# Scores issued ahead of the weighted values on TensorE, five copies of the values, and the key copy ahead of the logits' copy on ScalarE

## The chip, the cores and the metric

The kernel runs on one core of one Trainium2 chip. Its time is the device time in microseconds (us) of one execution; the median of three runs before the change is 304.14 us (303.58 to 305.31). The profile used below is of one execution of 303.86 us, whose first and last instruction lie 302.0 us apart.

## The reference

The kernel computes a gated cross-attention block followed by a gated mixture of eight experts, for 64 sequences of 64 rows of 128 numbers:

```
q = rope(layernorm(x) @ Wq.T + bq);  k = rope(ctx @ Wk.T + bk);  v = ctx @ Wv.T + bv      # 16 heads of 8
p = softmax(where(mask == 0, -1e9, q @ k.T / sqrt(8)))
x = x + tanh(g_xattn) * ((p @ v) @ Wo.T + bo)
y = layernorm(x);  logits = y @ Wr + br;  e = argmax(logits);  gate = softmax(logits)[e]
x = x + tanh(g_ffn) * gate * (gelu(y @ W1[e] + b1[e]) @ W2[e] + b2[e])
```

## The kernel before

**Tiling.** The 4096 rows are 32 tiles (T) of 128 rows, two sequences each. The attention of a tile is spread over seven steps of a software pipeline: every engine runs the same loop of steps, in step i it works on tile i for the projections and on older tiles for the later stages, and semaphores join the engines. Each engine executes its own list strictly in the order written in its `step(i)`; nothing reorders it. From step 34 on the expert layers follow, 39 sorted tiles of rows, gathered from a table in memory (`rows`).

**The stages of attention, with their lines.** In step i:

- TensorE (PE in the profile): projections of tile i (L763 to L765, `ps_qx` and `ps_kv`); transposes of the stacked queries and keys of tile i-1 (L778); weighted values of tile i-4, probabilities times values (L788, called pv below), into `ps_o`; scores of tile i-2 (L803), used only for the row maxima; transpose of the normalised output of i-5 (L815); the scores again, transposed and with the maxima taken off, of tile i-3 (L827 and L830, into `ps_st`); output projection of i-5 (L843, L844); transpose of the maxima of i-2 (L854). The projections of the next tile follow.
- VectorE (DVE): normalises the output of i-5 (L1144, L1147); queries with bias of tile i (L1157); residual and statistics of i-6 (L1172 to L1180); row maxima of the scores of i-2 (L1212, `mx`); splits the rotated queries and keys of tile i into halves (L1223, L1224, `stk`). Five groups of tiles are routed to experts in between (steps 11 to 14, 18 to 21, 25 to 28 and later).
- ScalarE (ACT): exponentials of i-4 (L589, `pr`); copy of the transposed maxima of i-3 (L595, `mxT`); copy of the router's part of tile i, eight columns (L605, the logits' copy); keys of tile i (L609, `qk`, the key copy); mask row (L613); keys and queries of i-1 out of PSUM (L623 `kT`, L626 `qT`); four copies of the values of tile i (L637, `vx`); output of i-5 (L643).
- GpSimd (POOL): the low halves of the stack of tile i-1 (L526); scatter of finished rows (L512, steps 15 to 31); the rotary embedding of tile i (L539, L541, L545).
- SyncE (SP): for tile i-1 four DMAs that copy `kT` into a block-diagonal form, `kbd` (L406). The scores L803 and L830 read `kbd`. SP also issues the input and weight loads (weights at steps 4, 7, ... 25, columns, context and rows at 3, 5, 6, 9 and so on), behind the four of the step.

**What joins them.** The scores of tile t wait for the four DMAs of `kbd` (`kbd_ld`), for `qT` and for the maxima of tile t-1 (`mx_done`, since `ps_s` is one buffer). pv of tile t waits for the exponentials (`p_rdy`), for the values (`v_ev`) and for the normalisation of tile t-1 (`on_done`). L778 waits for the halves of the stack (`hi_done`, `lo_done`) and for the copies of older maxima (`mxT_ev`). The exponentials wait for L830 (`st_done`). `kbd`, `qT` and `vx` are rings of four (`RING = 4`): the value copy of tile t waits until pv of tile t-4 is done.

Of the kernel before, what the change touches and what calls it, by code (L numbers as in the profile page):

```python
# [12 lines left out]
ACT = mybir.ActivationFunctionType  # L13
# [3 lines left out]
P = 128  # L17
B, S, D = 64, 64, 128
H, HD = 16, 8
T = B * S // P  # L20
NE, FF = 8, 512
FC = FF // P
NS = T + NE - 1
NA = 4
# [4 lines left out]
EPS = 1e-5  # L29
OUT_OF_RANGE = 8192  # L30
RING = 4
GOT = 20
W_SCALE = 64.0
QX = D + NE
ROW = 144
R_LOGIT, R_MEAN, R_VAR, R_STD, R_GATE, R_ID = 128, 136, 137, 138, 139, 140
# [54 lines left out]
def wait(eng, sem, n):  # L91

    if n > 0:
        eng.wait_ge(sem, n)
# [7 lines left out]
def build(nc, x, ctx_t, mask, g_x, g_f, Wq, bq, Wk, bk, Wv, bv, Wo, bo, W1, W1r, W2, b2, Wr, br,  # L102
          x_t, WoN, const_f, const_h, const_i, rows, out):
    stack = ExitStack()
    with stack:
        def sb(name, shape, dt=F32):
            return stack.enter_context(nc.sbuf_tensor(name, shape, dt))
# [56 lines left out]
        x_all = sb("x_all", [P, T, ROW])  # L164
# [12 lines left out]
        kT = sb("kT", [P, 2, NA, P], F16)  # L177
        qT = sb("qT", [P, RING, NA, P], F16)
        kbd = sb("kbd", [P, RING, 2, 2 * NA, 2, S], F16)
        vx = sb("vx", [P, RING, 2, 8, 32])  # L180
        mx = sb("mx", [P, 2, P], F16)
        mxT = sb("mxT", [P, 2, P], F16)
        pr = sb("pr", [P, 2, 8, 2, S])
# [50 lines left out]
        ps_s = ps[1]  # L234
# [7 lines left out]
        ps_lx = bank[6][:, D:QX]  # L242
# [69 lines left out]
        def live(t):  # L312
            return 0 <= t < T
# [257 lines left out]
        def _(act):  # L571
# [12 lines left out]
            def step(i):  # L584
# [16 lines left out]
                t = i  # L601
                if live(t):
                    par, s = t % 2, t % RING
                    act.wait_ge(qe_ev, t + 1)
                    act.activation(x_all[:, t, R_LOGIT:R_LOGIT + NE], ps_lx, ACT.Copy).then_inc(lx_ev, 1)  # L605
                    if t == 0:
                        act.wait_ge(s_mb, 2)
                    wait(act, rope2, t - 1)
                    act.activation(qk[:, par, D:2 * D], ps_kv[:, 0:D], ACT.Identity, scale=mask_s[:, t:t + 1]).then_inc(k_ev, 1)  # L609
                    if t == 0:  # L610
                        act.wait_ge(s_z1, 5)
                    wait(act, stk_done, t - 1)
                    act.activation(k_stack(par)[:, :, ROW_MASK], mask_b[:, t:t + 1].broadcast_to([P, H]), ACT.Copy  # L613
                                   ).then_inc(mrow, 1)
# [12 lines left out]
                                   ).then_inc(qT_ev, 1)  # L627
                t = i
                if live(t):
                    s = t % RING  # L630
                    wait(act, pv_done, t - RING + 1)
                    if t == 0:
                        act.wait_ge(s_v1, 2)
                    v_ps = ps_kv[:, D:2 * D].rearrange("p (j hh d) -> p j hh d", hh=2, d=HD)
                    for b in range(2):
                        for hh in range(2):
                            act.activation(vx[64 * hh:64 * hh + 64, s, b, :, 16 * hh:16 * hh + HD],  # L637
                                           v_ps[64 * b:64 * b + 64, :, hh, :], ACT.Copy).then_inc(v_ev, 1)
# [25 lines left out]
        def _(pe):  # L664
# [84 lines left out]
            def step(i):  # L749
# [17 lines left out]
                if live(t):  # L767
                    par = t % 2
                    pe.wait_ge(hi_done, 2 * t + 2)
                    pe.wait_ge(lo_done, t + 1)  # L770
                    pe.wait_ge(mrow, t + 1)
                    wait(pe, mxT_ev, t - 1)
                    wait(pe, qT_ev, t)
                    for w in range(2):
                        first = w * (H * STK + 8)
                        for a in range(NA):
                            c = (w * NA + a) * P
                            mm = pe.transpose(ps_stk[:, c:c + P], stk[:, par, first + a * P:first + a * P + P], ident_h)  # L778
                    mm.then_inc(stk_done, 1)
                t = i - 4  # L780
                if live(t):
                    s, par = t % RING, t % 2
                    pe.wait_ge(p_rdy, t + 1)
                    pe.wait_ge(v_ev, t * 4 + 4)
                    wait(pe, on_done, t)
                    for j in range(8):
                        for b in range(2):
                            mm = pe.matmul(ps_o[S * b:S * b + S, 32 * j:32 * j + 32], pr[:, par, j, b, :], vx[:, s, b, j, :],  # L788
                                           start=True, stop=True)
                    mm.then_inc(pv_done, 1)  # L790
                if tile(i - F0):
                    rows_transposed(i - F0)
                if tile(i - F0 - 1):
                    first_layer(i - F0 - 1)
                t = i - 2
                if live(t):
                    s = t % RING
                    pe.wait_ge(kbd_ld[s], (t // RING) * 64 + 64)
                    pe.wait_ge(qT_ev, t + 1)
                    wait(pe, mx_done, t)  # L800
                    for a in range(NA):
                        for b in range(2):
                            mm = pe.matmul(ps_s[S * b:S * b + S, 2 * P * a:2 * P * a + 2 * P], qT[:, s, a, S * b:S * b + S],  # L803
                                           kbd[:, s, :, 2 * a + b, :, :].rearrange("p w h k -> p w (h k)"),
                                           start=True, stop=True)
                    mm.then_inc(s_done, 1)
                t = i - 5
                if live(t):
                    if t == 0:
# [488 lines left out]
```

## Time and profile before

| | us |
|---|---|
| median of 3 runs | 304.14 (303.58 to 305.31) |
| profiled execution | 303.86 |
| its span, first to last instruction | 302.0 |
| TensorE busy | 238.8 (79%) |
| VectorE busy | 191.4 (63%) |
| ScalarE busy | 166.5 (55%) |
| GpSimd busy | 182.0 (60%) |
| mean granted TensorE clock | 0.955 |

The attention takes roughly the first 200 us and the experts the rest. In the full steps of attention (38 to 175 us) all four compute engines are busy for most of the time, so a step is set by chains that pass through several engines. Times in the views are from the span's start. A row of the timeline merges instructions of a line that follow each other (x8: eight of them); the brackets give the engine's idle time before it and what ended that.

### The profile page before, as it was taken

To read this page: it belongs to the slowest core of one execution; us is meant where nothing else is said; L and a number is where in the kernel's file an instruction comes from. 1 tells how busy PE (TensorE), PEld (TensorE's weight loads), DVE (VectorE), ACT (ScalarE), POOL (GpSimd) and SP (SyncE) were. 2 spreads that over 40 slices of the span, in tenths; PEclk is the share of its full clock that TensorE was granted. 3 is DMA by queue.
4 is the path that set the end of the run, shared out by engine and by line. 5 is a ranking of instruction groups with operands and counts; after the bars stand their busy time and mean duration, and the time that the engine had idled before them with its cause. 6 is when DMAs were issued, how large, how long until landed. Compare 5 with 4: busy or idle time off the path is not lost.

```text
span 302.0 us, 10491 instructions
## 1 busy us (share of the span) xinstructions
PE 238.8 (79%) x3529; PEld 207.8 (69%) x3529; DVE 191.4 (63%) x639; ACT 166.5 (55%) x481; POOL 182.0 (60%) x222
## 2 busy tenths in 40 slices
PE   1358889997998887888889967866676899999960
PEld 1236667876887676677677846755565899999960
DVE  5545858889898889977798684754452444444420
ACT  2145577887877875687786852352512444444410
POOL 7466665659468885488967766036473445555560
PEclk9999999999999999999999995799877999999995
DMA  7711465446454724143521212411134322200100
GB/s 221 218 17 25 103 177 124 125 114 185 108 136 114 200 59 135 25 126 66 137 46 37 47 36 71 109 33 40 59 107 112 100 65 61 74 29 31 37 19 0
DMA packets 58536, 26.63 MB, mean 88 GB/s; under 512 B 38609, under 2 KB 53990, under 8 KB 58485
## 3 DMA queue, kind: packets, MB, share of 16 engines
q1 hardware_dynamic: 55204, 20.15, 27.7%
q0 software_dynamic: 2272, 4.46, 4.4%
q10 hardware_dynamic: 1008, 1.35, 1.5%
q8 instruction: 31, 0.51, 0.7%
q14 instruction: 21, 0.16, 0.2%
HBM read 16.70 MB, written 5.51 MB: 74 GB/s over the span
## 4 chain that ended last, share of the span: by engine, by line
PE 35%; DVE 13%; POOL 13%; issue 12%; ACT 7%; SPq 6%; DMA 5%; another core or an unknown queue 4%; POOLq 1%; DVEq 0%; ACTq 0%
PE ps L745 11%; SPq L406 5%; PE ps L788 4%; DMA kbd<-kT 3%; POOL rot L545 3%; POOL rot L539 3%; POOL rot_s L541 3%; PE ps L728 2%; PE ps L726 2%; PE ps L727 2%; PE ps L803 2%; DVE mx L1212 2%; ACT pr L589 2%; DMA x_all<-in_x 2%
## 5 line engine op out<-in xcount | busy, mean ns | idle before, releaser
L560 POOL DMA_INDIRECT out<-fin,got x39 | 37.7, 967 | 37.5 <-DVE fin L1261 26.4
L1212 DVE TENSOR_REDUCE mx<-ps 128x16 f16<-128x1024 f32 x32 | 39.1, 1222 | 19.1 <-PE ps L803 15.1
L745 PE MATMUL ps<-w_f,hT 128*128 x312 | 46.8, 295 | 0.0
L512 POOL DMA_INDIRECT rows<-x_all,dest_i x32 | 33.3, 1040 | 21.4 <-DVE x_all L1062 14.3
L1261 DVE SCALAR_TENSOR_TENSOR fin<-ps,got 128x128 f32<-128x128 f32 x39 | 13.6, 350 | 46.9 <-PE ps L745 33.1
L788 PE MATMUL ps<-vx,pr 128*64 128x32 f32 x1024 | 37.3, 227 | 4.1 <-DVE on L1147 2.4
L745 PEld LDWEIGHTS ps<-w_f,hT 128*128 128x128 f32 x312 | 39.7, 199 | 0.8
L788 PEld LDWEIGHTS ps<-vx,pr 128*64 128x64 f32 x1024 | 33.8, 142 | 8.0 <-issue 2.9
L589 ACT ACTIVATE pr<-ps 128x1024 f32<-128x1024 f32 x32 | 32.7, 1023 | 8.7 <-PE ps L830 8.2
L539 POOL TENSOR_TENSOR rot<-qk,cf 128x256 f32<-128x256 f32 x32 | 23.5, 734 | 22.1 <-ACT qk L609 16.3
L657 ACT ACTIVATE hT<-ps 128x512 f32<-128x512 f32 x39 | 23.3, 597 | 23.2 <-PE ps L728 16.2
L526 POOL TENSOR_TENSOR stk<-rot,stk 128x256 f16<-128x256 f32 x32 | 21.6, 675 | 23.4 <-DVE stk L1224 23.4
L830 PE MATMUL ps<-qT,kbd 128*128 128x64 f16 x512 | 33.7, 195 | 0.7 <-issue 0.7
L827 PE MATMUL ps<-mxT,ch 128*128 128x128 f16 x256 | 33.7, 223 | 0.0
L830 PEld LDWEIGHTS ps<-qT,kbd 128*128 128x128 f16 x512 | 31.5, 100 | 1.5 <-issue 1.1
L778 PEld LDWEIGHTS ps<-ch,stk 128*128 128x128 f16 x256 | 16.0, 101 | 22.9 <-issue 18.4
L778 PE MATMUL ps<-ch,stk 128*128 128x128 f16 x256 | 20.7, 227 | 13.1 <-POOL stk L526 10.2
L726 PE MATMUL ps<-gT,w_h 128*128 128x128 f16 x156 | 30.0, 227 | 0.0
L727 PE MATMUL ps<-gT,w_h 128*128 128x128 f16 x156 | 29.9, 226 | 0.0
L728 PE MATMUL ps<-gT,w_l 128*128 128x128 f16 x156 | 29.8, 226 | 0.0
L637 ACT ACTIVATE vx<-ps 64x64 f32<-64x64 f32 x128 | 27.9, 218 | 2.5
L600 ACT ACTIVATE gT<-ps 128x128 f16<-128x128 f32 x39 | 10.8, 277 | 31.0 <-PE ps L714 23.4
(156 smaller groups left out, 604.6 us busy)
## 6 DMA issues: line engine op xcount, KB each, us to landing
kbd<-kT SPq DMA_DIRECT2D x128, 32.0 KB
got<-rows SPq DMA_DIRECT2D x39, 72.0 KB
w_f<-in_W_rows SPq DMA_DIRECT2D x8, 256.0 KB, 2.9
w_r<-in_W_last_row SPq DMA_DIRECT2D x8, 256.0 KB, 4.1
w_f<-in_L_ffn_W SPq DMA_DIRECT2D x8, 256.0 KB
x_all<-in_x SPq DMA_DIRECT2D x3, 512.0 KB, 4.7
xt_all<-in_x_t SPq DMA_DIRECT2D x3, 512.0 KB, 4.3
ct_all<-in_ctx SPq DMA_DIRECT2D x3, 512.0 KB, 4.3
```

The costliest lines, as they stand in the source:

```text
L512: pool.indirect_dma_start(out=rows, out_offset=bass.IndirectOffsetOnAxis(ap=dest_i[:, t:t + 1], axis=0), in_=x_all[:, t, :], in_offset=Non ...
L560: pool.indirect_dma_start(out=out_d, out_offset=bass.IndirectOffsetOnAxis(ap=got_i[:, u % GOT, R_ID:R_ID + 1], axis=0), in_=fin[:, u % FRI ...
L589: act.activation(pr[:, t % 2, :, :, :].rearrange("p j b q -> p (j b q)"), ps_st[:, :], ACT.Exp, scale=SCALE).then_inc(p_rdy, 1)
L726: pe.matmul(o, w_h, gT[:, par, 0, :], start=True, stop=False)
L727: pe.matmul(o, w_h, gT[:, par, 1, :], start=False, stop=False)
L728: mm = pe.matmul(o, w_l, gT[:, par, 0, :], start=False, stop=True)
L745: mm = pe.matmul(o, hT[:, par, c, :], w2_f[:, bass.ds(e, 1), c, :].rearrange("p o n -> p (o n)"), start=False, stop=(c == FC - 1))
L778: mm = pe.transpose(ps_stk[:, c:c + P], stk[:, par, first + a * P:first + a * P + P], ident_h)
L788: mm = pe.matmul(ps_o[S * b:S * b + S, 32 * j:32 * j + 32], pr[:, par, j, b, :], vx[:, s, b, j, :], start=True, stop=True)
L827: pe.matmul(ps_st[:, P * j:P * j + P], sel_h[:, j, :], mxT[:, par, :], start=True, stop=False)
L830: mm = pe.matmul(ps_st[:, c:c + S], kbd[:, s, j % 2, 2 * (j // 2) + b, :, :].rearrange("p h k -> p (h k)"), qT[:, s, j // 2, S * b:S * b + ...
L1212: dve.tensor_reduce(mx[:, t % 2, 0:H], ps_s[:, :].rearrange("p (h k) -> p h k", k=S), AX.X, ALU.max).then_inc(mx_done, 1)
```

## The change

Three edits. TensorE issues the scores of tile i-2 directly behind the transposes of tile i-1 and ahead of pv of tile i-4; the order of all else on it stays. The values get a ring of five buffers (`VRING = 5`), so that the copy of tile t waits for pv of tile t-5. ScalarE makes the key copy ahead of the logits' copy; the wait on `qe_ev` now stands ahead of the key copy.

```
+VRING = 5
-        vx = sb("vx", [P, RING, 2, 8, 32])
+        vx = sb("vx", [P, VRING, 2, 8, 32])
...
                     act.wait_ge(qe_ev, t + 1)
-                    act.activation(x_all[:, t, R_LOGIT:R_LOGIT + NE], ps_lx, ACT.Copy).then_inc(lx_ev, 1)
                     if t == 0:
                         act.wait_ge(s_mb, 2)
                     wait(act, rope2, t - 1)
                     act.activation(qk[:, par, D:2 * D], ps_kv[:, 0:D], ACT.Identity, scale=mask_s[:, t:t + 1]).then_inc(k_ev, 1)
+                    act.activation(x_all[:, t, R_LOGIT:R_LOGIT + NE], ps_lx, ACT.Copy).then_inc(lx_ev, 1)
...
-                    s = t % RING
-                    wait(act, pv_done, t - RING + 1)
+                    s = t % VRING
+                    wait(act, pv_done, t - VRING + 1)
...
+                t = i - 2
+                if live(t):
+                    s = t % RING
+                    pe.wait_ge(kbd_ld[s], (t // RING) * 64 + 64)
+                    pe.wait_ge(qT_ev, t + 1)
+                    wait(pe, mx_done, t)
+                    for a in range(NA):
+                        for b in range(2):
+                            mm = pe.matmul(ps_s[...], qT[...], kbd[...], start=True, stop=True)
+                    mm.then_inc(s_done, 1)
                 t = i - 4
                 if live(t):
-                    s, par = t % RING, t % 2
+                    s, par = t % VRING, t % 2
                     pe.wait_ge(p_rdy, t + 1)
...
-                t = i - 2
-                if live(t):
...
-                    mm.then_inc(s_done, 1)
```

On TensorE, one step of attention before the change, from the projections (`wqx`, `wkv`, `bk_h`) through the stack's transposes (`stk`), pv (`vx,pr`) and the scores (`kbd,qT`) to the transpose of the output (`on`):

```order
L763 MATMUL ps<-wqx,xt_all 128x136 [waits router_part_copied,v_copied]
L764 MATMUL ps<-wkv,ct_all 128x256
L765 MATMUL ps<-bk_h,ch 128x128
L778 MATMUL ps<-ch,stk 128x128 [waits max_copied,mask_row_made,qT_copied,lo_made,hi_made]
L778 MATMUL ps<-ch,stk 128x128 x7
L788 MATMUL ps<-vx,pr 64x32 [waits o_normalised,v_copied,probs_made]
L788 MATMUL ps<-vx,pr 64x32 x15
L803 MATMUL ps<-kbd,qT 64x256 [waits max_made,qT_copied,kbd_loaded3]
L803 MATMUL ps<-kbd,qT 64x256 x7
L815 MATMUL ps<-cf,on 128x128 [waits x2_made,o_normalised]
```

The same place after it (the lines are one higher, and the scores are now L789, pv is L801):

```order
L764 MATMUL ps<-wqx,xt_all 128x136 [waits router_part_copied,v_copied]
L765 MATMUL ps<-wkv,ct_all 128x256
L766 MATMUL ps<-bk_h,ch 128x128
L779 MATMUL ps<-ch,stk 128x128 [waits max_copied,mask_row_made,qT_copied,lo_made,hi_made]
L779 MATMUL ps<-ch,stk 128x128 x7
L789 MATMUL ps<-kbd,qT 64x256 [waits max_made,qT_copied,kbd_loaded3]
L789 MATMUL ps<-kbd,qT 64x256 x7
L801 MATMUL ps<-vx,pr 64x32 [waits o_normalised,v_copied,probs_made]
L801 MATMUL ps<-vx,pr 64x32 x15
L816 MATMUL ps<-cf,on 128x128 [waits x2_made,o_normalised]
```

The scores with their wait for the DMAs of `kbd` have moved ahead of the 16 products of pv; what stands in front of and behind the pair is the same.

On ScalarE, one step before the change, from the exponentials (`pr`) to the copies of the values (`vx`):

```order
L589 ACTIVATE pr<-ps 128x1024 [waits pv_made,scoresT_made]
L595 ACTIVATE mxT<-ps 128x128 [waits scoresT_made,max_transposed]
L605 ACTIVATE x_all<-ps 128x8 [waits q_scaled]
L609 ACTIVATE qk<-ps,mask_s 128x128 [waits rope_sin]
L613 ACTIVATE stk<-mask_b 128x16 [waits stacks_transposed]
L623 ACTIVATE kT<-ps 128x512 [waits kbd_loaded3,stacks_transposed]
L626 ACTIVATE qT<-ps 128x512 [waits scoresT_made]
L637 ACTIVATE vx<-ps 64x8x8 [waits pv_made]
```

And after it:

```order
L590 ACTIVATE pr<-ps 128x1024 [waits pv_made,scoresT_made]
L596 ACTIVATE mxT<-ps 128x128 [waits scoresT_made,max_transposed]
L609 ACTIVATE qk<-ps,mask_s 128x128 [waits rope_sin,q_scaled]
L610 ACTIVATE x_all<-ps 128x8
L614 ACTIVATE stk<-mask_b 128x16 [waits stacks_transposed]
L624 ACTIVATE kT<-ps 128x512 [waits kbd_loaded3,stacks_transposed]
L627 ACTIVATE qT<-ps 128x512 [waits scoresT_made]
L638 ACTIVATE vx<-ps 64x8x8 [waits pv_made]
```

The key copy (`qk`) and the logits' copy (`x_all`) have changed places; the copy of the values still waits for pv, now for that of the tile five back.

## Rows read from the trace of the kernel before

**Rows 1.** The page: busy us, share of the span, instructions by engine.
```profile
PE 238.8 (79%) x3529; PEld 207.8 (69%) x3529; DVE 191.4 (63%) x639; ACT 166.5 (55%) x481; POOL 182.0 (60%) x222
```

**Rows 2.** Stretches: length, busy time (x instructions) by engine, granted clock, DMA share, GB/s.
```profile
38.00:63.00 25.00, 22.46 (x408) 19.01 (x404) 19.69 (x61) 20.05 (x64) 15.02 (x21) 1.00 0.53 133
175.00:200.00 25.00, 19.08 (x329) 16.37 (x330) 16.42 (x63) 9.63 (x25) 8.58 (x11) 0.80 0.29 66
```

**Rows 3.** Timeline of one full step (start us, us, engine line).
```profile
62.50 0.61 PE L778 MATMUL ps<-ch,stk 128*128 128x128 f16 x8 [0.45 <-ACT mxT L595]
63.04 1.12 PE L788 MATMUL ps<-vx,pr 128*64 128x32 f32 x32
63.99 0.61 PE L803 MATMUL ps<-kbd,qT 128*64 128x256 f16 x8
...
65.81 1.02 ACT L589 ACTIVATE pr<-ps 128x1024 f32<-128x1024 f32 x1 [0.35 <-PE ps L830]
65.95 0.22 PE L854 MATMUL ps<-ch,mx 128*128 128x128 f16 x1
...
66.35 0.67 POOL L526 TENSOR_TENSOR stk<-rot,stk 128x256 f16<-128x256 f32 x1 [1.02 <-DVE stk L1224]
...
66.73 0.27 ACT L595 ACTIVATE mxT<-ps 128x128 f16<-128x128 f16 x1
66.76 0.22 PE L765 MATMUL ps<-bk_h,ch 128*128 128x128 f16 x1
...
67.26 0.44 PE L778 MATMUL ps<-ch,stk 128*128 128x128 f16 x5 [0.28 <-POOL stk L526]
```

**Rows 4.** Waits of 26 to 180 us: us in total, times, longest.
```profile
DVE mx L1212 <- PE ps L803: 12.7, 15, 1.4
ACT pr L589 <- PE ps L830: 5.8, 17, 0.4
PEld ps L803 <- DMA kbd<-kT: 2.6, 3, 1.2
PE ps L803 <- DMA kbd<-kT: 2.2, 2, 1.1
```

**Rows 5.** Timeline: a step whose scores wait for the DMAs.
```profile
102.90 0.61 PE L778 MATMUL ps<-ch,stk 128*128 128x128 f16 x8 [0.28 <-POOL stk L526]
...
105.70 0.63 PE L803 MATMUL ps<-kbd,qT 128*64 128x256 f16 x8 [1.13 <-DMA kbd<-kT]
...
108.98 0.22 PE L778 MATMUL ps<-ch,stk 128*128 128x128 f16 x1 [0.28 <-POOL stk L526]
```

**Rows 6.** The chain of waits near 20 us (start us, us): an issue, its landing, the scores.
```profile
20.60 1.98 DMA kbd<-kT
...
22.62 1.08 PE ps L803 x8
```

**Rows 7.** Timeline of SP: the four issues of kbd for tiles 7 and 9.
```profile
54.16 3.39 SPq L406 DMA_DIRECT2D kbd<-kT  x4
63.90 2.55 SPq L406 DMA_DIRECT2D kbd<-kT  x4
```

**Rows 8.** Timeline of TensorE: the scores of those two tiles.
```profile
59.06 0.61 PE L803 MATMUL ps<-kbd,qT 128*64 128x256 f16 x8
68.75 0.61 PE L803 MATMUL ps<-kbd,qT 128*64 128x256 f16 x8
```

**Rows 9.** Timeline of a step set by GpSimd (132 to 139 us).
```profile
132.19 0.67 POOL L526 TENSOR_TENSOR stk<-rot,stk 128x256 f16<-128x256 f32 x1 [0.61 <-DVE stk L1224]
132.96 0.61 PE L778 MATMUL ps<-ch,stk 128*128 128x128 f16 x8 [0.80 <-POOL stk L526]
...
137.29 0.66 POOL L526 TENSOR_TENSOR stk<-rot,stk 128x256 f16<-128x256 f32 x1
```

**Rows 10.** Timeline of the last scores of attention.
```profile
188.15 1.02 ACT L589 ACTIVATE pr<-ps 128x1024 f32<-128x1024 f32 x1 [1.18 <-PE ps L830]
...
189.26 1.92 PE L788 MATMUL ps<-vx,pr 128*64 128x32 f32 x32 [0.37 <-ACT pr L589]
...
190.96 1.07 PE L803 MATMUL ps<-kbd,qT 128*64 128x256 f16 x8
```

More of the change, by code:

```diff
@@ L779, in step @@
                     mm.then_inc(stk_done, 1)
+                t = i - 2
[6 more added lines that the diff above has]
+                        for b in range(2):
+                            mm = pe.matmul(ps_s[S * b:S * b + S, 2 * P * a:2 * P * a + 2 * P], qT[:, s, a, S * b:S * b + S],
+                                           kbd[:, s, :, 2 * a + b, :, :].rearrange("p w h k -> p w (h k)"),
+                                           start=True, stop=True)
+                    mm.then_inc(s_done, 1)
                 t = i - 4
                 if live(t):
-                    s, par = t % RING, t % 2
+                    s, par = t % VRING, t % 2
                     pe.wait_ge(p_rdy, t + 1)
@@ L794, in step @@
                     first_layer(i - F0 - 1)
-                t = i - 2
-                if live(t):
[L797 to L805, printed above, removed]
-                    mm.then_inc(s_done, 1)
                 t = i - 5
```

## The prediction

> **What bounds the kernel now.** I read the page's busy shares first [rows 1]: no engine fills the span, so a step of attention is set by a chain. The stretches [rows 2] then show where: TensorE is busy for 22.46 of 25 us between 38 and 63 us, and its clock is granted in full. Next the timeline of one undisturbed step [rows 3]: the transposes L778 start at 62.50 and again at 67.26, so a step is 4.76 us. Three chains lead from one to the other.
>
> Chain A, through ScalarE: L778, pv, scores and the transposed scores run back to back on TensorE until the exponentials can start at 65.81 (3.31 us). They end at 66.83, the copy of the maxima L595 behind them ends at 67.00, and L778 starts at 67.26: 3.31 + 1.02 + 0.17 + 0.26 = 4.76. The wait table confirms it: the exponentials waited for L830 17 times between 26 and 180 us [rows 4].
>
> Chain B, through VectorE and GpSimd: L778, pv, scores, maxima, the two halves of the stack, L526 (ends 67.02), L778. In the steps where L526 was the last thing waited for L778 comes 0.10 us behind its end (132.86, 132.96) [rows 9], so this chain needs 67.12 - 62.50 = 4.62 us [rows 3].
>
> Chain C is TensorE's own work: L778 at 62.50 to the end of L765 at 66.98, 4.48 us, including the 0.22 us that the last product drains.
>
> The timeline names L526 as the last releaser of L778 by 0.02 us, but both are within a hair; what matters is that A stands at the full 4.76.
>
> **Moving the scores.** It removes nothing and adds no instruction. In chain A both pv and scores lie between L778 and L830, in whichever order: the swap takes nothing out of it. In chain B pv drops out, 63.99 - 63.04 = 0.95 us; but B is only level with A, so while A stands the gain is between 0 and 4.76 - 4.62, and I take 0. The 15 waits of the maxima for the scores, 12.7 us [rows 4], look like the gain of this change; yet behind the maxima in many of those steps VectorE waits again, for the rotary embedding, and in the rest TensorE comes to the maxima's transpose L854 when its own list allows (65.95 above, 0.08 us behind the maxima's end).
>
> The price is the cover of a DMA. The scores wait for the four `kbd` transfers of their tile, and pv of an older tile, which needs none of them, was executed during that wait. An in-order TensorE now stands still with pv behind the wait; the output transpose, L830, the exponentials and the next L778 are all queued behind pv. In the step at 102.90 pv ran right behind L778 and the scores waited till 105.70, 1.13 us idle [rows 5]. With the swap the scores still start at 105.70, pv starts about 0.5 us later than them, and L830 comes 0.95 us later than before.
>
> How much cover each tile has left: a landing comes 1.37 us behind the end of its last issue at the least (20.60 + 1.98 = 22.58, the issue itself being 0.61 us) [rows 6]. For tile 9 the issues end at 66.45, so it has landed at 67.82, and the scores started at 68.75: 0.93 us to spare, just the 0.95 that is needed. For tile 7 the issues end at 57.55, landed 58.92, scores at 59.06: 0.1 us to spare [rows 7, 8]. The same subtraction for all tiles 2 to 29 gives six with nothing to spare (2, 4, 5, 11, 16, 22; five of these waits are visible, 4.8 us [rows 4]), three with 0.1 (7, 8, 27), ten with 0.4 to 0.98 (3, 6, 9, 13, 14, 15, 17, 23, 25, 28), and the rest with enough.
>
> What of it reaches the end. A stall lengthens its own step, and the next tile's `kbd`, issued relative to the step's start, then has that much more time; so 5 falls in the shadow of 4 and 8 in that of 7. The delays of L778 by tile: Tile 2: 0.95, of which about 0.45 lies in a step that waited for L526 and had that room: +0.5. Tiles 4, 11, 16: +0.75, +0.8, +0.95 = +2.5 (what tile 2 gave the next steps is taken off). Tile 5: +0.2. Tiles 7 and 27: 0.85 each, less 0.1 of room in the first: +1.65. Tile 22: 0.95, but steps 22 to 26 are set by GpSimd (scatter, rotary embedding, L526 in a ring of 137.29 - 132.19 = 5.1 us [rows 9], whatever TensorE does) and TensorE catches up: 0. The ten with partial cover: their missing parts come to about 2 us, most of it eaten by the room that an earlier stall made: +0.6.
>
> Together +5.45. The bounds of this term: only the visible waits outside the GpSimd-bound steps, four times 0.95 halved by room, 1.9 us; or all cover lost with nothing eaten, (6 x 0.95) + (3 x 0.87) + 2.0 = 10.3 us.
>
> The Trainium skill ("DMA: Bandwidth & Descriptors", Rules for kernel authors) says to issue a DMA early, compute, and wait on its semaphore late; this change waits earlier for the same issue. By that rule every transfer would lose cover, which is the upper bound, 10.3 us; the rows agree with it for tile 7 and leave tile 9 almost untouched [rows 7, 8], so the sum above stands.
>
> **The tail.** At 188.15 to 189.17 TensorE waits for the exponentials and then does pv and the scores of tile 31 (189.26, 190.96) [rows 10]. With the swap these scores run in the gap. They take 1.07 us there, at the lower clock; I take -0.9 us (0 to -1.07). The scores of tile 30 have landed too late to gain.
>
> **Five value buffers.** Before, pv ends at 64.16 just before the values' copy; with pv 0.5 us later a ring of four would make ScalarE wait that long in front of the value copies and the next projections. With five it waits for a pv a whole step old. So this edit removes a cost of the first one and gives nothing by itself: 0. The larger memset (one quarter more) lies in the start-up, and what it delays, GpSimd's zeroing of `kbd`, is needed only when the first `kbd` issue comes, many microseconds later: 0.
>
> **The key copy first.** The logits' copy holds ScalarE for about 0.07 us ahead of the key copy. GpSimd gets the keys 0.07 us earlier; where it was waiting for them and is on the path (about three steps) that gives -0.2 us. The logits' copy is needed by the next projections, behind the value copies on the same engine, so its delay costs 0.
>
> **Sum.** +5.45 - 0.9 - 0.2 = +4.35. VectorE's own long steps (routing; 102.90 to 108.98 is one of 6.1 us [rows 5]) will swallow a little more than I gave them; I take +4.0. On the profiled execution that is 303.86 + 4.0 = 307.9 us; the profiled time is 0.3 below the median of the runs, so I leave it at 307.9. The expert part is only shifted: its first tiles stand behind the last attention steps on every engine.
>
> **Rivals.**
> 1. The maxima's chain was the bound, and the stalls are small: A is only seemingly full (L595's 0.26 us to L778 could be a coincidence), B loses 0.95, and the step falls to chain C, 4.48. About 12 steps are at 4.76 to 4.83, so 12 x 0.28 = 3.4 us, and the tail 0.9. With stalls of 1.9 us: 303.86 - 3.4 - 0.9 + 1.9 = 301.5 us, faster. For it: L778's releaser is named L526 in this step, and the waits of the maxima are the largest on VectorE. Against it: the 17 waits of the exponentials [rows 4], and L778 never less than 0.25 us behind L595, 0.26 here [rows 3]. It decides from the point where the stalls come to less than about 2.8 us (303.86 - 4.3 + 2.8 is 1.8 below the median).
> 2. The stalls are hidden: the steps bound by VectorE and GpSimd swallow them all but two, and the tail gives back 0.9: 303.86 + 1.9 - 0.9 - 0.2 = 304.7 us, no change. For it: of 28 steps only about half are near 4.8 us.
> 3. All cover is lost, with late transfers made later by the longer queue: 303.86 + 10.3 - 1.1 = 313.1 us. Against: the shadowing above is plain arithmetic.
> 4. The clock falls. The step at 102.90 had 1.13 us of idle for `kbd` [rows 5], the longest such wait is 1.2 us [rows 4], and between 38 and 63 us the clock kept 1.00, while 175 to 200 us with its long waits has 0.80 [rows 2]. If two steps ran at the lower of the two levels (1.2 instead of 2.4 GHz), each would cost up to another 4.48 us: 307.9 + 9 = 317 us. [...]
>
> **Chances.** Forecast (3 to 6 us of loss) 0.6; rival 1 0.12; rival 2 0.15; rival 3 0.1; rival 4 0.03. A measurement here tells a change from none at about 0.5%, 1.5 us. Faster by more than that (under 302.6): 0.12. Within: 0.14. Slower (over 305.7): 0.74. The range 303.0 to 311.2 leaves out rival 1's 0.12 below, and rival 4 and part of rival 3 above. The forecast's own range is 305.7 to 310.
>
> **What would show it.** Right: the scores' waits for `kbd` grow from 4.8 us in 5 (26 to 180 us) to over 10 us in ten or more; pv follows the scores; the maxima's waits for the scores shrink to a few us while the exponentials still wait for L830 in about as many steps; undisturbed steps stay at 4.76. Steps at 4.5 us would show rival 1. The prediction is wrong if the pv that starts at 189.26 now [rows 10] starts no later than that.

## The result, and the profile after

On one chip, runs of the two kernels in turn: 308.6 us median after (306.25 to 309.22, 4 runs) against 303.86 before (302.93 to 305.31, 4 runs). The ratio is 1.0126, 95% interval 1.0076 to 1.0175, so the change costs 1.3%. Times in this document are medians of all runs and ratios compare the fast runs alone, which matters for the second timing of after: three of its six runs were slow, and it is 310.85 us over all six and 307.76 over the fast three. The profiled execution of after took 308.0 us (span 306.1, granted clock .943); that of before 303.86 (302.0, .955). A second pair of traces from another chip, called the repeats below, gives 309.54 against 304.71 us (spans 307.8 and 302.8).

The busy times of after, in the columns of [rows 1]:

```profile
PE 239.0 (78%) x3529; PEld 212.7 (69%) x3529; DVE 191.3 (62%) x639; ACT 164.6 (54%) x481; POOL 181.9 (59%) x222
```

As many instructions as before, and as busy, but for the weight loads (+4.9 us) and ScalarE (-1.9 us). The loss is waiting and clock. The wait table of after, 26 to 180 us, against [rows 4]:

```profile
PEld ps L789 <- DMA kbd<-kT: 13.4, 17, 1.4
ACT pr L590 <- PE ps L831: 9.8, 20, 0.9
PE ps L789 <- DMA kbd<-kT: 9.6, 13, 1.2
DVE mx L1213 <- PE ps L789: 4.0, 8, 1.0
```

The scores' wait for `kbd` has grown and the maxima's wait for the scores has shrunk, 12.7 to 4.0 us. These rows also show a mistake of mine: PEld and PE are the two halves of one stall (the load waits, and its matmul behind it), so they must not be added. Counted by the weight loads, before had 3 stalls of 2.6 us in all, not five of 4.8, and after has 17 of 13.4 us. The repeats say 3 of 1.4 and 15 of 10.7. Below I count by the weight loads alone, and call each such wait a stall.

One step with such a stall, that of tile 7's scores, against [rows 3] and the first row of [rows 8] (timeline of after; start, duration, engine line):

```profile
57.73 0.61 PE L779 MATMUL ps<-ch,stk 128*128 128x128 f16 x8 [0.31 <-ACT mxT L596]
...
59.27 0.63 PE L789 MATMUL ps<-kbd,qT 128*64 128x256 f16 x8 [0.93 <-DMA kbd<-kT]
...
59.73 1.07 PE L801 MATMUL ps<-vx,pr 128*64 128x32 f32 x32
59.94 1.23 DVE L1213 TENSOR_REDUCE mx<-ps 128x16 f16<-128x1024 f32 x1 [0.32 <-PE ps L789]
60.73 0.33 PE L816 MATMUL ps<-cf,on 128*128 128x128 f32 x1
...
62.01 1.02 ACT L590 ACTIVATE pr<-ps 128x1024 f32<-128x1024 f32 x1
62.93 0.27 ACT L596 ACTIVATE mxT<-ps 128x128 f16<-128x128 f16 x1
...
63.45 0.61 PE L779 MATMUL ps<-ch,stk 128*128 128x128 f16 x8 [0.31 <-ACT mxT L596]
```

TensorE stands for 0.93 us with pv queued behind the scores, and everything behind pv is that much later: from the transposes to the exponentials 62.01 - 57.73 = 4.28 us (3.31 in an undisturbed step of before), and the step takes 5.72 us instead of 4.76. The releaser of L779 is now ScalarE's copy of the maxima, in this step and in the undisturbed ones, which take 4.72 us.

The end of attention: the last scores (tile 31), with the exponentials and pv of their step (tile 29; timeline), against [rows 10]:

```profile
189.76 1.02 ACT L590 ACTIVATE pr<-ps 128x1024 f32<-128x1024 f32 x1 [1.18 <-PE ps L831]
```
```profile
190.43 1.06 PE L789 MATMUL ps<-kbd,qT 128*64 128x256 f16 x8
191.29 1.86 PE L801 MATMUL ps<-vx,pr 128*64 128x32 f32 x32
```

The scores of tile 31 do stand ahead of pv, but TensorE comes to them only at 190.43, 0.67 us behind the start of the exponentials, and pv then waits for nothing but its turn: 191.29 instead of 189.26.

How the two pairs part along the span. First the start of the last tile's transposes (timeline) in before and in its repeat:

```profile
180.51 0.61 PE L778 MATMUL ps<-ch,stk 128*128 128x128 f16 x8 [0.92 <-POOL stk L526]
```
```profile
179.96 0.61 PE L778 MATMUL ps<-ch,stk 128*128 128x128 f16 x8 [0.92 <-POOL stk L526]
```

and in after and in its repeat:

```profile
182.03 0.61 PE L779 MATMUL ps<-ch,stk 128*128 128x128 f16 x8 [0.85 <-POOL stk L527]
```
```profile
182.98 0.61 PE L779 MATMUL ps<-ch,stk 128*128 128x128 f16 x8 [0.85 <-POOL stk L527]
```

| us, after less before | first pair | repeats |
|---|---|---|
| last transposes of attention | +1.5 | +3.0 |
| from there to the end of the last exponentials | +0.2 | +1.7 |
| from there to the end of the span | +2.4 | +0.2 |
| span | +4.1 | +4.9 |

So 1.5 and 3.0 of the 4 to 5 us are lost by the last transposes, and the rest comes behind them. (The first transposes of after started 0.2 and 0.9 us earlier than those of before; counted from there, the attention steps cost 1.7 and 3.9 us.) The clock shows part of what comes behind. Stretches of the first trace of before (columns of [rows 2]):

```profile
202.00:230.00 28.00, 16.32 (x151) 14.73 (x151) 12.03 (x56) 9.00 (x19) 16.07 (x17) 0.88 0.22 68
230.00:240.00 10.00, 10.00 (x106) 9.89 (x106) 3.64 (x14) 3.78 (x9) 4.84 (x5) 0.83 0.46 118
```

and of the first of after:

```profile
202.00:230.00 28.00, 18.93 (x160) 17.02 (x159) 12.35 (x57) 9.34 (x18) 17.57 (x18) 0.82 0.20 64
230.00:240.00 10.00, 8.07 (x68) 7.98 (x68) 3.16 (x12) 3.28 (x8) 2.91 (x3) 0.66 0.38 102
```

In both stretches the first trace of after has less clock, 0.82 against 0.88 and 0.66 against 0.83. In the repeats it is another stretch, the end of attention itself; before, then after:

```profile
181.00:202.00 21.00, 16.91 (x270) 14.33 (x270) 12.69 (x51) 7.28 (x16) 6.46 (x7) 0.76 0.28 73
```
```profile
181.00:202.00 21.00, 17.52 (x222) 15.27 (x219) 11.75 (x43) 6.71 (x16) 6.71 (x7) 0.59 0.31 73
```

Between 184.6 and 201.6 us the repeat of after had the lower level, 1.2 GHz, without a break (the repeat of before from 182.4 to 192.6), and did 48 matmuls fewer in the 21 us.

### The profile page after: what moved, and what is told of

Read it like the earlier page. It is cut to its first block, busy times and chain, and to the rows that moved or that the text cites. A ratio compares the mean times of both kernels' runs of the same rounds, so it can differ in the third digit from the quotient of the medians.

```text
span 306.1 us, 10522 instructions
## 1 busy us (share of the span) xinstructions
PE 239.0 (78%) x3529; PEld 212.7 (69%) x3529; DVE 191.3 (62%) x639; ACT 164.6 (54%) x481; POOL 181.9 (59%) x222
## 3 DMA queue, kind: packets, MB, share of 16 engines
q10 hardware_dynamic: 1008, 1.35, 1.5%
## 4 chain that ended last, share of the span: by engine, by line
PE 45%; issue 12%; DMA 10%; SPq 9%; DVE 8%; ACT 6%; POOL 5%; another core or an unknown queue 2%; DVEq 0%; POOLq 0%; ACTq 0%
PE ps L746 13%; DMA kbd<-kT 8%; SPq L407 8%; PE ps L801 5%; PE ps L789 3%; PE ps L729 3%; PE ps L727 3%; PE ps L728 3%; PE ps L831 3%; PE ps L828 3%; ACT kT L624 2%; DVE mx L1213 2%; DMA x_all<-in_x 2%; PE ps L779 2%
## 5 line engine op out<-in xcount | busy, mean ns | idle before, releaser
L561 POOL DMA_INDIRECT out<-fin,got x39 | 37.8, 970 | 39.6 <-DVE fin L1262 29.1
L746 PE MATMUL ps<-w_f,hT 128*128 x312 | 48.9, 305 | 0.0
L746 PEld LDWEIGHTS ps<-w_f,hT 128*128 128x128 f32 x312 | 42.0, 209 | 0.8
L590 ACT ACTIVATE pr<-ps 128x1024 f32<-128x1024 f32 x32 | 32.7, 1023 | 13.4 <-PE ps L831 12.8
L801 PEld LDWEIGHTS ps<-vx,pr 128*64 128x64 f32 x1024 | 34.9, 141 | 1.5 <-ACT pr L590 1.5
L801 PE MATMUL ps<-vx,pr 128*64 128x32 f32 x1024 | 35.2, 223 | 0.9 <-ACT pr L590 0.9
L831 PE MATMUL ps<-qT,kbd 128*128 128x64 f16 x512 | 34.5, 197 | 1.0 <-issue 1.0
L779 PEld LDWEIGHTS ps<-ch,stk 128*128 128x128 f16 x256 | 16.0, 101 | 22.0 <-issue 18.2
L789 PE MATMUL ps<-kbd,qT 128*64 128x256 f16 x256 | 21.4, 292 | 12.2 <-DMA kbd<-kT 11.3
L779 PE MATMUL ps<-ch,stk 128*128 128x128 f16 x256 | 20.7, 227 | 12.2 <-POOL stk L527 5.5
```

Source lines behind the costliest of these rows:

```text
L561: pool.indirect_dma_start(out=out_d, out_offset=bass.IndirectOffsetOnAxis(ap=got_i[:, u % GOT, R_ID:R_ID + 1], axis=0), in_=fin[:, u % FRI ...
L590: act.activation(pr[:, t % 2, :, :, :].rearrange("p j b q -> p (j b q)"), ps_st[:, :], ACT.Exp, scale=SCALE).then_inc(p_rdy, 1)
L746: mm = pe.matmul(o, hT[:, par, c, :], w2_f[:, bass.ds(e, 1), c, :].rearrange("p o n -> p (o n)"), start=False, stop=(c == FC - 1))
L831: mm = pe.matmul(ps_st[:, c:c + S], kbd[:, s, j % 2, 2 * (j // 2) + b, :, :].rearrange("p h k -> p (h k)"), qT[:, s, j // 2, S * b:S * b + ...
```

## Experiments

Three groups of runs, each on one chip with the kernel before beside it. The chips are not equal: before took 288.78 us on the first, 304.2 on the second and 288.17 on the third, so only ratios, and the traces up to the end of attention, are carried from one to the other. "Last transposes" is the start of the last tile's, as above.

**The scores ahead, and nothing else.** The scores' block of before put ahead of pv; ring of four, logits' copy first.

```
@@ on TensorE, in the loop over i, behind the stack's transposes @@
+                t = i - 2
+                if live(t):
...                     (scores, as in the change)
                 (pv of tile i - 4)
-                t = i - 2
-                if live(t):
...
```

> The scores ahead of pv alone; ring of four and the logits' copy first, as before. Theory A (the scores' wait for kbd, with pv queued behind it, makes the loss; the ring of five takes away a second one): besides the kbd waits, ScalarE now waits for pv in front of the value copies, about 0.5 us, of which 0.15 to 0.3 us per undisturbed step comes through to the exponentials: last L778 at 183.5 to 186 us instead of 182.0, time 309.5 to 312. Rival (ring and key copy matter nothing): last L778 at 182 to 182.5, time 308 to 309.

Measured: 295.27 us, ratio 1.0231 (1.0188 to 1.0275). Last transposes:

```profile
184.23 0.61 PE L778 MATMUL ps<-ch,stk 128*128 128x128 f16 x8 [0.91 <-POOL stk L526]
```

Its waits, 26 to 180 us:

```profile
ACT vx L637 <- PE ps L800: 13.1, 24, 1.5
PEld ps L788 <- DMA kbd<-kT: 9.1, 15, 1.5
...
ACT pr L589 <- PE ps L830: 1.5, 1, 1.5
```

The move of the scores alone makes the loss, and more of it than the whole change (2.3% against 1.3 and 1.1%). The first row shows what the ring of five is for: with four, ScalarE's copies of the values wait for pv in 24 steps, 13.1 us, a row that does not exist in after. ScalarE becomes the late one, and TensorE almost never keeps the exponentials waiting (1 time instead of 17).

**Ring of five and key copy first, scores behind pv.** The changed kernel with the block put back.

```
@@ against the changed kernel @@
-                t = i - 2           (scores, ahead of pv)
...
                 (pv of tile i - 4)
+                t = i - 2           (scores, behind pv)
...
```

> The ring of five and the key copy first, the scores behind pv as before. Theory A: the kbd waits go back to 5 to 7 in number, last L778 at 180 to 180.5 us, time 303 to 304, as before or up to 0.5 us less. Rival B (the loss comes from the ring's memory or from ScalarE's order): last L778 at 181.5 or later, time 307 to 309.

Measured: 288.99 us, ratio 0.9982 (0.9943 to 1.0022). Waits, 26 to 180 us:

```profile
DVE mx L1213 <- PE ps L804: 13.8, 16, 1.7
...
PEld ps L804 <- DMA kbd<-kT: 2.7, 5, 0.7
```

No change in time that can be told, and nearly the wait table of before. The two smaller edits are neither loss nor gain together; the loss comes with the order of scores and pv.

**The changed order without the wait for `kbd`.** The scores of a tile read the block-diagonal keys of the tile before and wait for those, which have long landed (so the scores computed are another tile's).

```
@@ against the changed kernel @@
-                    pe.wait_ge(kbd_ld[s], (t // RING) * 64 + 64)
+                    o = max(t - 1, 0)
+                    r = o % RING
+                    pe.wait_ge(kbd_ld[r], (o // RING) * 64 + 64)
...
-    kbd[:, s, :, 2 * a + b, :, :]
+    kbd[:, r, :, 2 * a + b, :, :]
```

> The changed kernel, but the scores of tile t read the kbd of tile t-1 and wait for its landing, a step old (the maxima are those of other keys; all transfers are still made). Theory A: no wait for kbd in front of the scores, so the gains stay alone (2.8 us by the steps that got shorter, and 0.9 in the tail) with undisturbed steps at 4.72: last L778 at 176 to 178 us, time 299 to 302. Rival C (the wait is not the cost, pv being later in the step is): last L778 still at 181 to 182.5, time 307 to 309. Should the undisturbed step fall to 4.5 us, the maxima's chain was the bound after all.

Measured: 285.41 us, ratio 0.9865 (0.9821 to 0.9909). Last transposes, and one step (timeline):

```profile
176.59 0.61 PE L779 MATMUL ps<-ch,stk 128*128 128x128 f16 x8 [0.85 <-POOL stk L527]
```
```profile
60.58 0.61 PE L779 MATMUL ps<-ch,stk 128*128 128x128 f16 x8 [0.31 <-ACT mxT L596]
61.12 0.63 PE L791 MATMUL ps<-kbd,qT 128*64 128x256 f16 x8
61.58 1.07 PE L803 MATMUL ps<-vx,pr 128*64 128x32 f32 x32
...
63.85 1.02 ACT L590 ACTIVATE pr<-ps 128x1024 f32<-128x1024 f32 x1 [0.42 <-PE ps L833]
64.78 0.27 ACT L596 ACTIVATE mxT<-ps 128x128 f16<-128x128 f16 x1
...
65.30 0.61 PE L779 MATMUL ps<-ch,stk 128*128 128x128 f16 x8 [0.31 <-ACT mxT L596]
```

With the wait gone the same order is 1.35% faster than before instead of about 1.2% slower. So the loss comes from the wait for the DMAs in this order. But the step is 4.72 us, not 4.48: chain A is the bound, and rival 1's idea that TensorE alone would set the step is out.

**The same in the order of before.** The control for the run just told: the same edit, in before.

> The kernel before, scores behind pv, but reading the kbd of the tile one older and waiting for that landing (as in the third experiment). Theory A: the kernel before had most waits covered by pv, so this removes at most its 4.8 us of visible waits, of which 1 to 3 us reach the end: last L778 at 177.5 to 179.5 us, 0.3 to 1 per cent faster. Then the scores ahead of pv without a wait (176.6) are still ahead of it by 1 to 3 us, the gain of the order alone. Rival: the order gains nothing without the wait, and this kernel too ends its last L778 at 176.6.

Measured on the second chip: 303.42 us, ratio 0.9977 (0.9945 to 1.0009). Last transposes:

```profile
179.42 0.61 PE L778 MATMUL ps<-ch,stk 128*128 128x128 f16 x8 [0.92 <-POOL stk L526]
```

Before hardly loses anything by `kbd`. Against 179.42 the new order, freed of the wait, starts its last transposes at 176.59, 2.8 us earlier; I had taken that gain as 0. But it can't be put down to the order: four single steps are together 3.5 us shorter, and each has another reason in the traces. Two of them, 1.1 us together, stand at the start. TensorE is granted the higher clock level from 29.1 us here, and from 23.0 us in the run with the scores ahead. The transposes of tile 2, here and there:

```profile
26.44 1.06 PE L778 MATMUL ps<-ch,stk 128*128 128x128 f16 x8
```
```profile
25.93 0.61 PE L779 MATMUL ps<-ch,stk 128*128 128x128 f16 x8
```

The order is not what raises the clock: after has it from 29.2 us, and a run below whose first tiles are all in the order of before has it from 23.5. The third step, 1.55 us, holds a fall of the clock in this run, from 73.5 to 76.9 us (the step takes 6.28 us, in before and its repeat 4.81):

```profile
70.00:75.00 5.00, 3.33 (x53) 2.42 (x52) 3.93 (x13) 3.02 (x11) 4.11 (x5) 0.85 0.50 129
```

The fourth, 0.9 us, is told in the last section. So the two ratios, 0.9865 and 0.9977, say, each against before on its own chip, that without the wait the changed kernel is about 1% better; how much of that is the order's own is open.

**The repeats.** Both kernels unchanged, on the second chip.

> The kernel before itself, for its trace beside the other three. Last L778 at 180 to 181 us; the end wherever the granted clock and the transfers of this chip put it.

> The changed kernel itself, timed once more beside the kernel before on one chip. Theory A: last L778 1 to 2 us later than in the kernel before, ratio 1.004 to 1.016. Rival D (the first comparison's last 2.6 us, behind the attention, belong to the change too): ratio 1.012 or more, with the end 3.5 us or more later than before.

Measured: 304.71 us for the traced run of before (median of its 17 other runs 304.2); after 307.76, ratio 1.0106 (1.0047 to 1.0165). The ratio is in the expected range; the last transposes, 3.0 us later than in before, are not (1 to 2 expected). Waits of the repeat of before, 26 to 180 us:

```profile
DVE mx L1212 <- PE ps L803: 11.3, 15, 1.2
PEld ps L803 <- DMA kbd<-kT: 1.4, 3, 0.7
```

and of the repeat of after:

```profile
PEld ps L789 <- DMA kbd<-kT: 10.7, 15, 1.3
...
DVE mx L1213 <- PE ps L789: 3.0, 7, 0.7
```

The pattern is stable, single steps are not. The step with tile 4's scores went from 5.97 to 5.50 us in the first pair and from 5.31 to 5.65 in the repeats; the step that ends with the transposes of tile 26 from 4.80 to 5.05 and from 4.79 to 6.09.

**The scores ahead only where the transfer has landed.** Tiles whose landing left room in before go ahead of pv, the others stay behind.

```
@@ against the changed kernel; scores(t) is its block made a function @@
+            FIRST = (6, 9, 10, 12, 15, 18, 19, 20, 21, 24, 26, 29, 30, 31)
...
+                if live(i - 2) and i - 2 in FIRST:
+                    scores(i - 2)
                 (pv of tile i - 4)
+                if live(i - 2) and i - 2 not in FIRST:
+                    scores(i - 2)
```

> The changed kernel, with the scores ahead of pv only for tiles 6, 9, 10, 12, 15, 18 to 21, 24, 26 and 29 to 31, whose kbd had landed 0.9 us or more before the scores in the kernel before; behind pv for the others. Theory A: hardly a loss (under 0.5 us), part of the gain: last L778 at 178.5 to 180 us, time 301 to 303.5. Rival C: half of the loss stays, last L778 at 181, time 305 to 307.

> The fourth experiment's kernel again (scores ahead of pv only for the fourteen tiles whose kbd is early), beside the kernel before on one chip. Theory A: last L778 1.5 to 2.5 us earlier than before, ratio 0.990 to 0.998.

Measured: 287.62 us, ratio 0.9958 (0.9921 to 0.9994), on the first chip, and 286.92, 0.9972 (0.9938 to 1.0007), on the third. Waits of the first, 26 to 180 us, and its last transposes:

```profile
DVE mx L1220 <- PE ps L760: 8.6, 12, 1.4
PEld ps L760 <- DMA kbd<-kT: 4.1, 7, 1.2
```
```profile
178.28 0.61 PE L794 MATMUL ps<-ch,stk 128*128 128x128 f16 x8 [0.84 <-POOL stk L527]
```

The loss is gone and some 0.3 to 0.4% is gained, at the edge of what can be told from nothing: the fastest version in which each tile's maxima come from its own scores, if only just. Attention gained more than that: the last transposes start at 178.28 here and at 176.50 in the second trace (1.5 to 2.5 us earlier than in before was expected, 3.5 to 4.0 came). Yet the last exponentials end at 192.06 and 192.08 us. In the second trace VectorE waits for the first rows that were gathered for the experts, and the normalisation that pv needs stands behind that wait in its list:

```profile
186.09 0.34 DVE L1139 TENSOR_SCALAR z<-got 128x127 f32<-128x127 f32 x1 [1.03 <-DMA got<-rows]
```

So an attention that ends early can be held up by the next stage's transfers. How much of the 1.8 us between the two traces went that way was not tested.

**Are the loads of the experts' second weights why `kbd` comes late?** SP issues them in the same steps. One step later (against the changed kernel):

```
+                if i - 1 in EXPERT_AT:
+                    e = EXPERT_AT[i - 1]
                     sp.dma_start(w2_f[:, e, :, :], ...
```

> The changed kernel, with the second layer's weights (256 KB each, the last of three loads that SP issues behind kbd in steps 4, 7, ... 25) issued one step later. Theory A: kbd of tiles 4, 7, 10, 13, 16, 22 lands late because these loads fill the queue; a third of them moved away makes those landings up to 1 us earlier, but the next tile's later: waits for kbd fall from 23 us to 17 to 21, last L778 at 180.5 to 181.8 us, time 0 to 1.5 us less than the changed kernel. Rival: landings are late for SP's own issue time (2.5 to 3.4 us for four), then nothing changes.

Measured: 310.65 us, ratio 1.0217 (1.0174 to 1.0259); 15 stalls, 12.2 us; last transposes at 184.09. Not better than the changed kernel on that chip (1.0106) but worse, so this expectation failed. Why it is worse was not found; its trace also has the lower clock level from 76.6 to 80.0 us, which after does not. Then all of them behind attention, in the changed kernel and in the selective one:

```
-                    sp.dma_start(w2_f[:, e, :, :], ...
...
+                if i == T:
+                    for e in range(NE):
+                        sp.dma_start(w2_f[:, e, :, :], ...
```

> The changed kernel, with all eight loads of the second layer's weights issued in step 32, behind the last kbd. A third of the bytes of the weight loads is then gone from steps 4 to 25 instead of moved by a step. If these loads make kbd land late (theory A): waits of the scores for kbd from 20 to 26 us down to 12 to 18, last L778 at 180 to 181.5 us; the total is open, since 2 MB now land while the first gathered rows do. Rival: SP's issue time alone makes kbd late, then waits stay within 1 us of the changed kernel and last L778 is at 182 to 183.

> Both together: scores ahead of pv for the fourteen tiles, second layer's weights at step 32. Last L778 at 176.5 to 178.5 us; ratio to the kernel before 0.985 to 0.997, if the late weights don't hold the first expert tiles up; if they do, 1.00 to 1.01.

Measured: 298.01 us, ratio 1.0377 (1.0321 to 1.0433), and 294.34, ratio 1.022 (1.0169 to 1.027). The times say little: SP now issues these loads ahead of the first gathers of rows for the experts, and in the first of the two VectorE waits 6.1 us for the first of those rows. The second was expected at 0.985 to 0.997, or at 1.00 to 1.01 if the experts were held up; it came out worse than both. The waits of the first, 26 to 180 us, and its last transposes:

```profile
PEld ps L791 <- DMA kbd<-kT: 10.8, 17, 1.1
```
```profile
180.56 0.61 PE L781 MATMUL ps<-ch,stk 128*128 128x128 f16 x8 [0.84 <-POOL stk L529]
```

With none of those loads in attention there are still 17 stalls, 10.8 us (after 17 and 13.4, its repeat 15 and 10.7). So these loads are not why TensorE stalls. The last transposes come 1.5 and 2.4 us earlier than in after and its repeat, which is what the expectation wanted to see if the loads did matter; 0.9 us of that is again the step of the last section. In 12 of the 17 stalls `kbd` landed 1.34 to 1.36 us behind the end of its last issue, about the shortest time seen: there the cover is short by the issue and the landing of `kbd` themselves. In the other five it landed 1.6 to 2.7 us behind, and why was not found. Tile 9 in before: its transposes start at 62.50 [rows 3], its four issues are the quickest there are, 2.55 us to 66.45 [rows 7], and land 1.37 us later, at 67.82: 5.32 us. Scores ahead of pv come one step and 0.54 us behind the transposes, 4.72 + 0.54 = 5.26 us. So the new order has no room at all in an undisturbed step, and there every issue slower than 2.55 us, and every later landing, stalls TensorE.

**Does a delay late in attention cost more than itself?** Before, with the scores of tile 28 made five times over (same values).

```
@@ against before @@
+                    for _ in range(5 if t == 28 else 1):
                         for a in range(NA):
...
```

> The kernel before, with the eight score matmuls of tile 28 made five times instead of once: 32 more matmuls, 1.84 us more on TensorE in one step of attention and no other change. It asks what a delay at the end of attention costs in the total. If the expert part is only shifted: last L778 1.4 to 1.9 us later, the total 1.4 to 2.2 us more (ratio 1.005 to 1.007). Rival D (a later attention also makes the transition and the clock's windows cost more): total 2.8 us or more (ratio 1.009 or more).

Measured: 290.37 us, ratio 1.008 (1.0045 to 1.0115), that is +2.3 us (1.3 to 3.3) for a step that grew from 4.76 to 6.50, +1.74 us. Both expectations overlap the interval: neither is excluded, and other steps of its trace were longer too (its last transposes start at 183.50, 3.0 us later than in before, and its clock was at the lower level from 75.9 to 79.3 us). That a lost us late in attention costs more than one stays open.

## Why the prediction was right, step by step

The total was right: 307.9 forecast, 308.6 measured on the first chip and 307.76 on the other, both inside 303.0 to 311.2. So was the mechanism: the cover of the `kbd` transfers is lost. Its terms were not all right, and that they sum to the right total is partly luck, as errors cancelled: attention was priced too dear, what lies behind it at nothing.

- **The removed cover.** Shown. Scores alone: 1.0231. Without the wait: 0.9865. All nine tiles named with no more than 0.1 us to spare (2, 4, 5, 7, 8, 11, 16, 22, 27) wait in the trace of after and in its repeat; of the ten with partial cover 13, 14, 17, 23, 25 and 28 wait too in the first, and beside them 20 and 29. Subtracting the landing from the start of the scores, tile by tile, is a good forecast of who waits. Two things it had too simple. 1.37 us from the last issue to the landing is about the least (1.34), not the rule: tiles 4, 5, 16 and 17 landed 2.3 to 3.6 us behind it in before, and the prediction's own list holds only with their real landings. And the move is 0.95 us only where pv starts at once. In the step of tile 29's scores pv itself had waited for VectorE in before, 1.27 us up to 176.19, so these scores moved forward by about 2.2 us, and a tile that was counted as safe waits in both traces of after.
- **The wait rows.** Mis-read: "five of these waits are visible, 4.8 us" was three, 2.6 us, shown twice. It entered only the lower bound: by its own rule three times 0.95 halved, 1.4 us instead of 1.9.
- **+5.45 for attention** was too much. By tiles, first pair: the step of tile 2 +0.47 (forecast +0.5), of 7 +0.80 and of 27 +0.79 (together +1.65 forecast, +1.59 measured), 4 and 5 together +0.13 (+0.95), 16 -0.35 (+0.95), 22 +0.29 (0). The step of 11 grew by 0.85 as forecast (0.8), but nearly all of it for another reason (last section). All steps that grew add to +4.6 us, and those that shrank to -2.9; I had no term for the second. Much of it is a step's scatter from run to run: the runs without the wait differ by 2.8 us, but the single long steps that make it up (the second 5.45 to 4.78 us, the third 5.19 to 4.78, the twelfth 6.28 to 4.73, the one of tile 25's scores 6.08 to 5.18) go with the clock and with the collision of the last section, not with the order. Undisturbed steps go only from 4.76 to 4.72. Chain B's saving of 0.95 us was priced in the undisturbed step and taken as 0 everywhere; what it is worth in the long steps is open. Net, attention lost 1.5 us in one pair and 3.0 in the other, not 4.55.
- **The tail, -0.9.** Wrong. I took the length of the exponentials, 1.02 us, for a gap on TensorE; but TensorE itself had stood for only 0.37 us there, as the pv row of [rows 10] says. Scores of 1.06 us do not fit into it: pv starts 2.03 us later than before, 1.5 of it the later attention. Measured for the stretch: +0.2 and +1.7.
- **"The expert part is only shifted."** Wrong: +2.4 us in the first pair behind the last exponentials, and in the repeats +0.2 there and the lower clock inside the tail. Part of it is rival 4 in small: it gave a clock loss 3% and placed it in the attention steps, but it came at the transition to the experts, where the clock was at its lower level in places already. (Inside attention the clock fell in four of the other traces, two of them without the new order; in neither trace of after did it fall there.) The extra time there goes along with the extra stretches at 1.2 GHz in both pairs; that they cause all of it is not shown.
- **Ring of five: 0; key copy first: -0.2.** Together 0.9982 (0.9943 to 1.0022), in line with both; and that a ring of four would make ScalarE wait is shown by the 13.1 us of the first experiment.
- **Rival 1** (steps of 4.5 us) fell: 4.72 without any wait. **Rival 2** (hidden) fell by its size, though some stalls were hidden as it says: in the first pair the steps of tiles 4 and 16 did not grow, though both tiles stalled. **Rival 3** (all cover lost, 313.1) did not come.
- **The tests named.** Stalls 3 to 17, exponentials' waits 17 to 20, maxima's 12.7 to 4.0 us, pv's last start 189.26 to 191.29: all as written, apart from the double count, with which 4.8 us in 5 became 23.0 in 30.

## What to carry to other kernels

Before a consumer is moved forward on an in-order engine, subtract for each tile the landing of its transfer (its own, not the shortest one seen) from the start of the consumer now: where less is left than the move, the engine stands, and all that is queued behind it with it. Take the move from the place where the consumer will stand: it is longer where the work that it passes was itself waiting. An order need not be all or nothing: moving only the tiles with room kept the small gain and none of the loss. And a long wait row (12.7 us of the maxima here) is no gain to be had while another chain is level with it; count a DMA stall of TensorE by one of its two rows. Before a difference between two traces is booked to an edit, look at each step that carries it: here four single steps made 3.5 us that belonged to the clock and to a collision of two engines.

## What the hardware did that I had not expected

**A VectorE instruction of 0.18 us can take 0.75.** The candidates of the routing (`cand`, 128x48, two inputs in SBUF) in the same step, in the repeat of before:

```profile
79.47 0.18 DVE L1003 SCALAR_TENSOR_TENSOR cand<-ldif,cf 128x48 f32<-128x48 f32 x1
79.48 0.75 POOL L541 TENSOR_TENSOR rot_s<-qk,cf 128x256 f32<-128x256 f32 x1
```

and in the kernel with ring and key copy alone:

```profile
79.73 0.73 POOL L542 TENSOR_TENSOR rot_s<-qk,cf 128x256 f32<-128x256 f32 x1
79.78 0.74 DVE L1004 SCALAR_TENSOR_TENSOR cand<-ldif,cf 128x48 f32<-128x48 f32 x1
```

Where VectorE is first by 0.01 us both run at their own length; where GpSimd is first by 0.05 us, VectorE ends at 80.52, just behind GpSimd's 80.46. The order of the two goes with the key copy, which comes 0.07 us earlier in the changed kernel: in all nine traces with the key copy first the instruction takes 0.73 to 0.75 us, in the five others 0.17 or 0.18. (The ring of five is in the same nine and was not tried apart.) The step went from 4.98 to 5.66 us there (5.62 in the run without the wait, 5.83 in after). That is nearly all of the +0.85 I had booked to tile 11's transfer. The Trainium skill ("SBUF — State Buffer", Who interferes with whom) says that a VectorE instruction with two SBUF inputs and a GpSimd instruction that reads SBUF exclude each other for a whole instruction, and that who is first decides; this trace agrees on VectorE's side, 0.18 against 0.74 us (that GpSimd waits when VectorE is first, its 0.75 us do not show).

The same instruction explains a second step, the one of tile 25's scores. In before, then in the first selective run, which has these scores behind pv as before has:

```profile
155.25 1.15 DVE L1003 SCALAR_TENSOR_TENSOR cand<-ldif,cf 128x56 f32<-128x56 f32 x1
```
```profile
153.58 0.36 DVE L1011 SCALAR_TENSOR_TENSOR cand<-ldif,cf 128x56 f32<-128x56 f32 x1
```

In before GpSimd had started 0.36 us earlier (154.89), and VectorE ended just behind its second operation; in the selective run GpSimd started 0.24 us later than VectorE. In the nine traces where this instruction takes 1.02 to 1.15 us the step takes 6.06 to 6.08, in the five where it takes 0.35 or 0.36 (without the wait, both selective runs, both with the weights last) 5.17 or 5.18. So an edit that shifts two engines against each other by a few tenths of a us can move a step by 0.7 to 0.9 us either way, which no sum of terms foresees.

**Chips differ by 5% on the same kernel**, 288.2 to 288.8 against 304.2 us, and nearly all of it behind attention: the last transposes begin between 176 and 184 us whatever the chip, and from the first to the sixth output tile of the experts it is 14 to 15 us on one kind and 21 on the other. TensorE's clock goes with it: between 180 and 240 us the ring-and-key kernel had the lower level for 6.8 us (182.6 to 186.0, 213.3 to 216.7), before on the dearer chip for 20.5. Which of the two causes the other was not found.
